# Moving the light heads' elementwise products from GpSimd to VectorE in a fused MoE, attention, MoE kernel

## The chip, the cores and the metric

The kernel runs on one core of a Trainium2 chip. Its metric is device time in microseconds (us) from the start to the end of one execution. TensorE is PE in the rows (PEld its weight loads), VectorE is DVE, ScalarE is ACT, GpSimd is POOL, SyncE is SP.

## The reference

The input x has 8 batches of 512 rows of 128 channels. Three residual stages follow one another:

```python
x = x + 0.5 * ffn(layernorm(x))      # 8 experts of 512 hidden units, the best one of each row
x = x + attention(layernorm(x))      # 16 heads of 8 channels, values are the keys, gated
x = x + 0.5 * ffn(layernorm(x))

windows = [max(4, 128 // 2 ** h) for h in range(16)]
mask = (j <= i) & (j > i - windows[h])
att = softmax(where(mask, q @ k.T / sqrt(8), -inf))
combined = att @ v                   # v = k
gates = softmax(x @ Wgate + bgate)   # one gate for each head
out = (combined * gates) @ Wproj + bproj
```

Head h looks back over a window of 128, 64, 32, 16, 8, 4, 4, ... keys. The four widest are called dense and the twelve others light.

## The kernel before

The program is one block with an instruction stream for each engine; their order is written out by hand and semaphores connect them. An expert stage sorts the rows by expert (scatter by indirect DMAs from GpSimd's queue, L481), computes 46 blocks of 128 rows in pairs (`ffn`, L1258 and L1267), and brings the rows back.

The attention stage goes through 8 batches of 4 tiles, and each batch i through 7 slots n, written here as slot (i, n). The dense heads go through TensorE: scores of unit n (L1343, L1345), negated maximum on VectorE (`dense_max`, L973 and L977), exponentials on ScalarE (L691, L694), transposes (L1355), copy (L704) and products with the values (`outputs`, L1370 to L1377). TensorE and VectorE work two units ahead of the slot (`ahead(i, n, 2)`), so VectorE's maximum in slot (i, 0) is that of unit (i, 2).

The light heads do not use TensorE. The keys of a batch are written to DRAM and loaded back four rows' shifts at a time into `ks` and four more for the widest light head into `ks4` (SP, `keys`). Then:

- `light_products` (L325) multiplies the shifted keys with the queries: a small one for `ks4` (L332, 128x128) and a large one for `ks` (L334, 128x1536). It waits for the load of the keys and for `lsc_s` of the batch before, after which `prod` is free.
- `light_sums` (L980) and `light_scores` (L992) reduce the products to scores on VectorE, `light_probs` (L707, L710) takes the exponential on ScalarE.
- `light_parts` (L337) multiplies the shifted keys with these probabilities (L341, L345), the same two sizes. `light_outputs` (L1012) sums them (L1015 to L1019), and `gate` (L1022) scales all heads (L1026 to L1042) for the projection. TensorE's `outputs(i, 0)` of the next batch waits for `gated_s` from `gate`, as its bank is read there.

Before the change GpSimd runs `light_products` for batches 1 to 7 and `light_parts` for batches 0 to 6; VectorE runs `light_products` of batch 0 and `light_parts` of batch 7 itself. GpSimd's share of the attention stage is `window(i)`, in order: `light_products(i)`; `roots` (L528) in windows 1 and 3; `normalise_batch(i + 2)` (L322), which needs TensorE's `turn_batch(i + 1)` of slot (i, 0) (L1307); in window 1 `centre` and `squares` of tiles 20 to 31 (L514, L509), after VectorE's means in slot (1, 2); in windows 3 to 6 `roots` and `normalise` (L528, L356); in window 2 `add_output_bias` (L522, 128x2560); and `light_parts(i)`.

VectorE's slots are in `slot_of` (L1070): in slot (i, 0) the maximum, from batch 2 on row sums and centring of batch i - 2 (L797, L807), then `light_outputs(i - 1)`; in slot (i, 1) the maximum and `gate(i - 1)`; in slot (i, 3), or (7, 2) in the last batch, the maximum and `light_sums(i)`; in slot (i, 4) maximum, `add_bias` and `light_scores(i)`. `besides` holds single pieces of work for some slots; the routing of the last expert stage is computed in slots (6, 4), (6, 6) and (7, 1) (L861 to L909), and the scatters of that stage wait for it.

Of the kernel before, what the change touches and what calls it, by code (L numbers as in the profile page):

```python
# [5 lines left out]
B, T, C = 8, 512, 128  # L6
# [58 lines left out]
def macaron(nc, x_in, w_qkg, b_qkg, w_q4, w_k4, b_q4, b_k4, w_proj, b_proj, w_router, w_fc, w_out, consts, out):  # L65
# [4 lines left out]
    with ctx:  # L70
# [3 lines left out]
        def sem(name):  # L74
            return ctx.enter_context(nc.semaphore(name))
# [140 lines left out]
        norm_s = sem("rows_normalised")  # L216
# [64 lines left out]
        def batch(i):  # L281
            return slice(4 * i, 4 * i + 4)
# [182 lines left out]
        def _(pool):  # L465
# [62 lines left out]
                pool.tensor_tensor(rstd[:, tiles], var[:, tiles], minus_half[:, 0:len_of(tiles)], ALU.pow).then_inc(root_s, 1)  # L528

            def window(i):  # L530
                if i > 0:
                    light_products(pool, i, i % 2)
                if i in (1, 3):
                    roots(i // 2 + 1, LN2[i // 2 + 1])
                if i + 2 < B:
                    normalise_batch(pool, i + 2)
                if i == 1:
                    centre(LN2[2])
                    squares(6, LN2[2])
                if 3 <= i < 7:  # L540
                    roots(i, batch(i - 3))
                    normalise(pool, 1, (root_s, i), batch(i - 3))
                if i == 2:
                    add_output_bias(6, slice(LN2[1].start, N_TILES))
                if i + 1 < B:
                    light_parts(pool, i, i % 2)

            pool.wait_ge(zero_s, 48)
            scatter(0, 0, SEG[0][0], 1)
# [237 lines left out]
        def _(dve):  # L787
# [58 lines left out]
            def spread(n, tiles):  # L846
                root_guess(n, tiles)
                for k in range(3):
                    root_step(tiles, last=k == 2)
# [203 lines left out]
            def half_attended(i):  # L1053
# [2 lines left out]


            besides = {
                (0, 2): lambda: light_products(nc.vector, 0, 0),
                (0, 0): lambda: residual(LN2[1], 4), (0, 1): lambda: row_sums(LN2[1]), (0, 3): lambda: centre(LN2[1]),  # L1060
                (0, 5): lambda: variance(5, LN2[1]), (0, 6): lambda: scaled_variance(5, LN2[1]),
                (1, 1): lambda: residual(LN2[2], 5), (1, 2): lambda: (row_sums(LN2[2]), means(LN2[2])),
# [7 lines left out]
            def slot_of(i, n):  # L1070
                nxt = ahead(i, n, 2)
                if nxt:
                    dense_max(*nxt)
                if i >= 2 and n == (0 if i + 1 < B else 4):

                    half_attended(i - 1)
                    row_sums(batch(i - 2))
                    if i == 2:

                        dve.wait_ge(cent_s, len(LN1) + len(LN2))  # L1080
                    centre(batch(i - 2))
                if i:
                    if n == 0:
                        light_outputs(i - 1)
                    if n == 1:
                        gate(i - 1)
                    if n == 6:
                        attended(i - 1)

                early = i + 1 == B  # L1090
                if n == 3 - early:
                    light_sums(i)
                if i + 1 < B:
                    if n in (2, 4):
                        add_bias(i + 1, n // 2 - 1)
                    if n == 5:
                        gate_logits(i + 1)
                if n == 4 - early:
                    light_scores(i)
                if i >= 2:  # L1100
                    if n == (4 if i == 2 else 2) and i + 1 < B:
                        variance(7 + i - 2, batch(i - 2))
                    if n == (6 if i == 2 else 5) and i < 6:
                        scaled_variance(7 + i - 2, batch(i - 2))
                if (i, n) in besides:
                    besides[i, n]()
# [69 lines left out]
            last = SEG[1][1]  # L1176

            spread(11, batch(4))
            normalise(nc.vector, 1, (rstd_s, len(SEG[0]) + 2), batch(4))
            gate(B - 1)  # L1180
            half_attended(B - 1)
# [353 lines left out]
```

## Time and profile before

| | |
|---|---|
| median of 3 runs | 498.62 us (497.4 to 502.13) |
| the profiled execution's own time | 496.32 us |
| its span, first to last instruction | 494.5 us |
| busy, of the span | PE 83%, DVE 67%, ACT 58%, POOL 48% |
| mean granted TensorE clock | 0.886 of full speed |
| attention stage | about 143 to 383 us |

Busy shares are averages over stages with different limits, so the attention stage is read by itself: the chain of waits shows what was waited for, and the timelines of each engine show which instruction took longer than others of its form. The times in a timeline are microseconds from the start of the span.

### The profile page before, as it was taken

Reading aid. Unit: us, or ns where it says so; the run is one execution under the profiler, and the core shown is the slowest. Engines: PE = TensorE matmul, PEld = TensorE weight load, DVE = VectorE, ACT = ScalarE, POOL = GpSimd, SP = SyncE. Lnnn points to the kernel's source line nnn. Section 1 sums busy time; section 2 is a strip of 40 time slices with the busy share of each in tenths; the row PEclk is TensorE's granted clock in tenths of the full one; section 3 lists DMA queues with packets and bytes.
Section 4 is the critical chain, followed back from the end, with each engine's and each line's share of the span. In section 5 each row is a group of like instructions: output and inputs, shape, how many; then the busy total and the mean of one; then the engine's idle time right before and its main releaser. Section 6 shows DMA issues by size and latency. Waiting matters only on the chain.

```text
span 494.5 us, 9979 instructions
## 1 busy us (share of the span) xinstructions
PE 408.2 (83%) x2828; PEld 381.5 (77%) x2837; DVE 330.3 (67%) x668; ACT 285.0 (58%) x875; POOL 235.2 (48%) x204
## 2 busy tenths in 40 slices
PE   2941999999977869959998989794887979989990
PEld 1940899999966868849797979693776969989990
DVE  5867344558754898895959696969894385545550
ACT  2330576767746647836868677753342746767660
POOL 4047760170227894651826252414375246777551
PEclk9999999999999767987979898876565799999997
DMA  8981332242216660522525322122023613362210
GB/s 254 407 227 59 98 115 64 77 125 74 64 34 136 138 158 13 124 50 64 109 63 110 81 70 74 15 50 37 33 98 105 179 36 107 104 177 63 62 42 0
DMA packets 85356, 48.16 MB, mean 97 GB/s; under 512 B 45874, under 2 KB 80314, under 8 KB 85073
## 3 DMA queue, kind: packets, MB, share of 16 engines
q1 hardware_dynamic: 80272, 37.32, 29.2%
q0 software_dynamic: 5056, 10.52, 6.8%
q8 instruction: 12, 0.20, 0.2%
q14 instruction: 16, 0.12, 0.1%
HBM read 25.66 MB, written 22.98 MB: 98 GB/s over the span
## 4 chain that ended last, share of the span: by engine, by line
PE 56%; DVE 20%; POOL 8%; issue 7%; ACT 3%; DMA 3%; POOLq 0%; DVEq 0%; SPq 0%; ACTq 0%
PE bank L1258 17%; PE bank L1267 17%; PE bank L1345 5%; POOL late_rows_d L481 4%; PE bank L1377 4%; DVE osh L1017 3%; PE bank L1326 3%; POOL rows_d L481 3%; PE bank L1249 2%; ACT late L694 2%; PE bank L1355 2%; DVE nmax L977 2%; PE bank L1233 2%; DMA xs<-late_rows_d 1%; DVE osh L1019 1%
## 5 line engine op out<-in xcount | busy, mean ns | idle before, releaser
L1267 PE MATMUL bank<-wo,hT 128*128 x736 | 101.6, 281 | 5.3 <-ACT hT L616 5.2
L915 DVE TENSOR_SCALAR hT<-bank 128x512 f32<-128x512 f32 x92 | 63.6, 691 | 59.5 <-PE bank L1258 58.9
L1258 PE MATMUL bank<-xT,fcb 128*128 128x128 f32 x736 | 101.1, 282 | 0.7 <-ACT xT L600 0.7
L1267 PEld LDWEIGHTS bank<-wo,hT 128*128 128x128 f32 x736 | 90.3, 193 | 6.6 <-issue 6.1
L1258 PEld LDWEIGHTS bank<-xT,fcb 128*128 128x128 f32 x736 | 93.2, 199 | 1.5 <-ACT xT L600 1.5
L610 ACT ACTIVATE fcb<-fc 128x512 f32 x92 | 57.7, 629 | 51.1 <-PE bank L1258 50.9
L616 ACT ACTIVATE hT<-hT 128x512 f32<-128x512 f32 x92 | 57.6, 626 | 10.1 <-DVE hT L915 9.9
L491 POOL DMA_INDIRECT out_rows<-late x46 | 45.3, 984 | 37.2 <-DVE late L924 30.4
L694 ACT ACTIVATE late<-bank,nmax 128x128 f32<-128x128 f32 (+1 forms) x128 | 50.0, 394 | 14.5 <-DVE nmax L977 13.6
L1345 PE MATMUL bank<-kT,qT 128*128 128x128 f32 (+4 forms) x256 | 54.2, 345 | 0.5
L704 ACT ACTIVATE PT<-bank 128x384 f32<-128x384 f32 (+1 forms) x56 | 28.6, 511 | 42.2 <-PE bank L1355 42.1
L1345 PEld LDWEIGHTS bank<-kT,qT 128*128 128x128 f32 x256 | 47.6, 219 | 3.2 <-issue 0.5
L977 DVE TENSOR_REDUCE nmax<-bank 128x1 f32<-128x256 f32 (+1 forms) x96 | 29.2, 345 | 31.1 <-PE bank L1345 30.4
L481 POOL DMA_INDIRECT rows_d<-rows,slot x32 | 32.5, 1016 | 34.2 <-DVE slot L909 25.1
L500 POOL DMA_INDIRECT late<-y_d,slot x32 | 32.0, 1000 | 35.0 <-DMA y_d<-ys 23.3
L481 POOL DMA_INDIRECT late_rows_d<-rows,slot x32 | 31.6, 986 | 27.5 <-DVE slot L909 18.4
L1233 PEld LDWEIGHTS bank<-wr,rT 128*128 128x128 f32 x128 | 28.5, 301 | 14.1 <-ACT rT L594 12.2
L1343 PE MATMUL bank<-maskb,identb 128*128 128x448 bf16 (+1 forms) x48 | 17.7, 369 | 25.5 <-ACT late L694 25.4
L600 ACT ACTIVATE xT<-bank 128x128 f32<-128x128 f32 x92 | 23.8, 261 | 18.3 <-PE bank L1249 18.2
L341 POOL TENSOR_TENSOR part<-ks,pl 128x128 f32<-128x128 f32 x7 | 3.0, 426 | 65.9 <-ACT pl L710 65.9
L1355 PE MATMUL bank<-cst,late 128*128 128x128 f32 x176 | 33.9, 311 | 0.0
L1377 PE MATMUL bank<-qkg,PT 128*128 128x8 f32 x192 | 33.6, 296 | 0.0
(133 smaller groups left out, 804.3 us busy)
## 6 DMA issues: line engine op xcount, KB each, us to landing
ks<-k_d SPq DMA_DIRECT2D x32, 192.0 KB, 3.3
late_rows_d<-hT SPq DMA_DIRECT2D x5, 1028.0 KB, 7.0
rows_d<-late SPq DMA_DIRECT2D x2, 1472.0 KB
xs<-rows_d SPq DMA_DIRECT2D x23, 128.0 KB
y_d<-ys SPq DMA_DIRECT2D x46, 64.0 KB
xs<-late_rows_d SPq DMA_DIRECT2D x23, 128.0 KB
late<-late_rows_d SPq DMA_DIRECT2D x2, 1225.5 KB, 6.9
fc<-in_w_fc SPq DMA_DIRECT2D x1, 2048.0 KB
```

The lines of the kernel that those rows point to most:

```text
L481: pool.indirect_dma_start(out=(late_rows_d if f else rows_d)[:, :], out_offset=bass.IndirectOffsetOnAxis(ap=slot[:, t:t + 1].bitcast(u32), ...
L491: pool.indirect_dma_start(out=out_rows, out_offset=bass.IndirectOffsetOnAxis(ap=xid[:, b, C:C + 1].bitcast(u32), axis=0), in_=xid[:, b, 0: ...
L610: act.activation(fcb[:, v, :], fc[:, ds(e, 1), :].rearrange("p e h -> p (e h)"), ACT.Copy)
L616: act.activation(block_h, block_h, ACT.Square).then_inc(hT_s, 1)
L694: act.activation(rows[:, to + 128 - w:to + 128], s[:, a0:a0 + w], ACT.Exp, bias=nmax[:, t, h:h + 1], accum_out=den[:, i % 2, t, h:h + 1]). ...
L915: nc.vector.tensor_scalar(hT[:, v, :, :].rearrange("p k c -> p (k c)"), bank[v][:, :], 0.0, None, ALU.max).then_inc(r_s, 1)
L977: mx = nc.vector.tensor_reduce(nmax[:, t, h:h + 1], s[:, a0:a0 + w], AX.X, ALU.max, negate=True)
L1258: mm = pe.matmul(bank[v][:, k * 128:(k + 1) * 128], fcb[:, v, k * 128:(k + 1) * 128], xT[:, v, :], start=True, stop=True)
L1267: mm = pe.matmul(bank[OUT_BANK[f] + v][:, 0:128], hT[:, v, k, :], wo[:, ds(e, 1), k, :], start=(k == 0), stop=(k == KT - 1))
L1345: mm = pe.matmul(s[:, a0:a0 + w], qT[:, u, h, t * 128:(t + 1) * 128], kT[:, u, (t + 1) * 128 - w:(t + 1) * 128], start=False, stop=h == he ...
L1355: mm = pe.transpose(bank[3][:, c * 128:(c + 1) * 128], P[:, (n + 1) // 2 % 2, k, :], ident)
L1377: mm = pe.matmul(o(h, h + 1), PT[:, t % 2, h + 1, :], v(t, h), start=(t == 0), stop=(t == 0 or h == DENSE - 1))
```

## The change

VectorE runs `light_products` and `light_parts` for all 8 batches. `light_products(i)` stands in slot (i, 3), or (7, 2), right ahead of `light_sums(i)`, and that of batch 0 moves from slot (0, 2) to (0, 3). `light_parts(i - 1)` stands in slot (i, 0), right ahead of `light_outputs(i - 1)`. GpSimd's windows lose both calls; everything else in them keeps its order. One wait on `norm_s` is added after the attention loop on VectorE.

```diff
             def window(i):
-                if i > 0:
-                    light_products(pool, i, i % 2)
                 if i in (1, 3):
                     roots(i // 2 + 1, LN2[i // 2 + 1])
                 if i + 2 < B:
@@
                 if i == 2:
                     add_output_bias(6, slice(LN2[1].start, N_TILES))
-                if i + 1 < B:
-                    light_parts(pool, i, i % 2)
@@
             besides = {
-                (0, 2): lambda: light_products(nc.vector, 0, 0),
@@
                 if i:
                     if n == 0:
+                        light_parts(nc.vector, i - 1, (i - 1) % 2)
                         light_outputs(i - 1)
@@
                 if n == 3 - early:
+                    light_products(nc.vector, i, i % 2)
                     light_sums(i)
@@
             spread(11, batch(4))
+            dve.wait_ge(norm_s, 6)
             normalise(nc.vector, 1, (rstd_s, len(SEG[0]) + 2), batch(4))
```

## Rows read from the trace of the kernel before

**Rows 1.** Page, chain that ended last, by engine
```profile
PE 56%; DVE 20%; POOL 8%; issue 7%; ACT 3%; DMA 3%; POOLq 0%; DVEq 0%; SPq 0%; ACTq 0%
```

**Rows 2.** Busy time by stretch, batches 2, 5, 6: us, busy (count), PEclk, DMA share, GB/s
```profile
204.50:236.00 31.50, 25.14 (x155) 22.87 (x156) 26.24 (x41) 18.39 (x74) 14.23 (x7) 0.84 0.34 75
...
283.20:307.00 23.80, 21.60 (x147) 19.33 (x147) 19.42 (x39) 17.73 (x71) 10.20 (x8) 0.93 0.26 60
307.00:343.60 36.60, 29.43 (x171) 25.93 (x171) 31.34 (x54) 19.27 (x75) 13.99 (x9) 0.78 0.25 50
```

**Rows 3.** Timeline of TensorE in batch 5
```profile
284.71 0.60 PE L1307 MATMUL bank<-cst,xb 128*128 128x128 f32 x4
...
293.97 0.36 PE L1371 MATMUL bank<-qkg,PT 128*128 128x8 f32 x2 [0.69 <-DVE fcb L1042]
```

**Rows 4.** Timeline of VectorE in batch 5, in brackets the idle time before
```profile
288.88 1.27 DVE L1019 TENSOR_TENSOR osh<-osh,o 128x32 f32<-128x32 f32 x1
...
300.31 0.54 DVE L977 TENSOR_REDUCE nmax<-bank 128x1 f32<-128x160 f32 x2 [2.15 <-PE bank L1345]
```

**Rows 5.** Source lines of three small VectorE instructions, eight of each
```profile
L1019 DVE TENSOR_TENSOR osh<-osh,o x8: 192/654/2726, 185.3 to 365.9; 128x32 f32<-128x32 f32 x8
L1037 DVE TENSOR_TENSOR fcb<-osh,fac x8: 557/558/1282, 189.1 to 371.1; 128x384 f32<-128x384 f32 x8
L1030 DVE TENSOR_TENSOR dg<-den,gsum x8: 224/226/5090, 188.0 to 370.0; 128x64 f32<-128x64 f32 x8
```

**Rows 6.** Timeline of GpSimd in batch 5
```profile
286.64 3.46 POOL L334 TENSOR_TENSOR prod<-ks,qkg 128x1536 f32<-128x1536 f32 x1
...
292.16 1.06 POOL L356 TENSOR_TENSOR rows<-rows,rstd 128x512 f32<-128x512 f32 x1
```

**Rows 7.** Source lines of the large products on both engines: duration ns min/median/max, starts
```profile
L334 POOL TENSOR_TENSOR prod<-ks,qkg x7: 3440/3462/3509, 181.4 to 337.7; 128x1536 f32<-128x1536 f32 x7
L334 DVE TENSOR_TENSOR prod<-ks,qkg x1: 1748/1748/1748, 163.5 to 163.5; 128x1536 f32<-128x1536 f32 x1
```

**Rows 8.** Timeline of VectorE, parts of batch 7: start us, us, instruction
```profile
360.03 0.29 DVE L341 TENSOR_TENSOR part<-ks,pl 128x128 f32<-128x128 f32 x1
360.23 1.75 DVE L345 TENSOR_TENSOR part<-ks,pl 128x1536 f32<-128x1536 f32 x1
```

**Rows 9.** Timeline of VectorE in slots (1, 3), (1, 4) and (1, 5)
```profile
194.43 0.68 DVE L977 TENSOR_REDUCE nmax<-bank 128x1 f32<-128x256 f32 x2
...
197.84 0.54 DVE L977 TENSOR_REDUCE nmax<-bank 128x1 f32<-128x160 f32 x2 [0.37 <-PE bank L1345]
...
200.52 0.68 DVE L973 TENSOR_REDUCE nmax<-bank 128x4 f32<-128x512 f32 x1
```

**Rows 10.** Timeline of VectorE, the centring of slot (5, 0)
```profile
284.35 0.69 DVE L807 SCALAR_TENSOR_TENSOR rows<-rowsum,rows 128x512 f32<-128x512 f32 x1
```

**Rows 11.** Timeline of VectorE, the maximum of slot (1, 1)
```profile
186.93 0.69 DVE L977 TENSOR_REDUCE nmax<-bank 128x1 f32<-128x256 f32 x2 [1.47 <-PE bank L1345]
```

**Rows 12.** Timeline of GpSimd in batches 1 and 2
```profile
194.60 2.76 POOL L514 TENSOR_TENSOR rows<-rows,rowsum 128x1536 f32<-128x1536 f32 x1 [7.00 <-DVE rowsum L801]
197.44 2.75 POOL L509 TENSOR_TENSOR sq<-rows 128x1536 f32<-128x1536 f32 x1
...
212.37 5.20 POOL L522 TENSOR_TENSOR rows<-rows,bproj 128x2560 f32<-128x2560 f32 x1
```

**Rows 13.** Timeline of ScalarE, first exponential of unit (2, 0)
```profile
202.08 0.36 ACT L694 ACTIVATE late<-bank,nmax 128x128 f32<-128x128 f32 x1
```

**Rows 14.** Timeline of VectorE, slots (2, 6), (6, 5) and (6, 6)
```profile
234.87 1.20 DVE L844 TENSOR_SCALAR var<-var 128x4 f32<-128x4 f32 x1
...
332.67 2.87 DVE L1006 TENSOR_TENSOR gl<-qkg,gmax 128x64 f32<-128x64 f32 x1
...
337.98 3.28 DVE L880 TENSOR_TENSOR n_tok<-upto,before 128x8 f32<-128x8 f32 x1
```

**Rows 15.** Timeline of GpSimd, an indirect DMA while VectorE ran L334
```profile
164.05 1.98 POOL L500 DMA_INDIRECT late<-y_d,slot  x1 [0.30 <-issue]
```

## The prediction

> **What bounds the kernel now.** I read the page's chain first, then the chain of waits through the attention stage, then the timelines of four engines side by side, batch by batch. The chain is TensorE for 56% and VectorE for 20% [rows 1]. The expert stages hold nothing that the change touches, so only the stretch from about 143 to 383 us can move. There an undisturbed batch takes 23.6 to 23.8 us; batch 2 takes 31.5 and batch 6, with the routing in it, 36.6 [rows 2]. In batch 5 TensorE is busy 21.6 us of 23.8 and VectorE 19.4 [rows 2]: neither is free, and they alternate. VectorE carries the chain from the maximum of slot (i, 0) to the end of `gate` in slot (i, 1), without a pause; TensorE carries it from `outputs(i, 0)`, which had waited 0.69 us for `gate` [rows 3], through slot (i, 4), where VectorE idles 2.15 us for it [rows 4].
>
> The reader should also see that VectorE's small instructions are sometimes very long. L1019 takes 0.19 us at best and 2.73 at worst, L1030 takes 0.22 and once 5.09, L1037 takes 0.56 or 1.28 [rows 5]. Each long one ends where a GpSimd instruction ends: L1019 at 290.15 [rows 4] with L334 at 290.10 [rows 6]. So an instruction with two tensors in SBUF waits on VectorE for GpSimd's running one. The Trainium skill has this as a rule (SBUF — State Buffer, section "Who interferes with whom"): the pair of ports is an exclusive lock, and whoever starts first keeps it for the whole instruction. The trace agrees, with 1.27 us for the L1019 at 288.88 where 0.19 is its least.
>
> **The change part by part.** GpSimd loses 7 large products L334 of 3.46 us [rows 7] and 7 somewhat shorter L345, with their small ones. It is not on the chain except in the scatters, so this time is itself worth nothing; what counts is what it blocked.
>
> VectorE gains 14 pairs. A pair costs 0.2 us for the small one (360.03 to 360.23) and 1.75 for the large one, 1.95 us [rows 8]; L334 is 1.75 there too [rows 7]. That is 27 us of work on VectorE. The seven `light_parts` stand in slot (i, 0), inside the stretch that carries the chain, and count in full. The seven `light_products` stand in slot (i, 3): where VectorE idles 2.15 us afterwards [rows 4] they are hidden (without that cover each would cost 1.95); batch 1 has only 0.37 us [rows 9] and the last batch next to none.
>
> GpSimd's other work moves forward. Its `normalise_batch` now starts as soon as `turn_batch` ends, at 285.31 in batch 5 [rows 3], and would find VectorE's large L345 running since about 285.2 (the centring L807 ahead ends near 285.0 [rows 10], plus 0.2 for L341). It waits, then runs under the reductions L1015 to L1017, which take one tensor and were not lengthened anywhere. With L528 and L356 behind it (some 3.1 us together) it is through before L1019. So in the batches without other work both L1019 and L1037 run at their shortest.
>
> The running sum, as delay of the chain:
>
> - Batch 0: products only change places in the row, 0. The parts of batch 0 in slot (1, 0) fill an idle time of 1.47 us ahead of the maximum of slot (1, 1) [rows 11]; the 0.5 us left over is taken up by ScalarE's and TensorE's own order.
> - Batch 1, slot (1, 3), +5.4. VectorE's means release GpSimd's L514, 2.76 us, 0.17 us after the start of the last maximum before the products [rows 9, 12]. That maximum has 0.6 us to go, so L332 finds the ports taken. With VectorE 0.5 us late it waits from 195.5 to 197.8. Behind L514 stands L509, 2.75 us [rows 12]. If it takes the ports between L332 and L334, the products end near 202.5, the maximum of unit (1, 6) starts at 204.7 where it had 197.84, and that of (2, 0) at 206.9 where it had 200.52 [rows 9]. The first exponential of (2, 0) had 0.9 us to spare (202.08 against 201.20) [rows 9, 13]: 6.3 less 0.9 is 5.4. If L334 goes ahead of L509, the same working gives 3.8. I take 5.4, since L509 has by then waited longer.
> - Batch 2, -1.0. Before, L1019 lost 1.08 us and L1030 4.87 to L334 and to the bias of 5.20 us [rows 5, 12]. Now the bias follows `normalise_batch` and ends 7.8 us after `turn_batch`; L1019 loses about 2.4 and L1030 nothing. Parts 1.95 plus 2.4 less 5.95 is -1.6. TensorE, at its lower clock of 1.2 GHz after some 4 us of idle time in batch 1, brings `turn_batch` and so the bias 0.6 us later: -1.0.
> - Batch 2, clock, -0.9. At a granted clock of 0.84 it had 25.14 us of matmuls [rows 2]; at batch 5's 0.93 these would be 22.7, so up to 2.4 us can come back when the single 4.8 us wait for L1030 is gone. TensorE would still idle near 1.7 us there, more than the 0.69 of batch 5 [rows 3], so I take a good third, 0.9.
> - Batch 3, +1.0: parts 1.95, less 0.95 of the 1.20 us of L844, which waited for GpSimd's L345 [rows 14]; TensorE's scores allow no more.
> - Batch 4, +0.4, and batch 5, +0.2: the maximum of slot (i, 1) comes 1.95 later less L1019's 1.1, and 0.69 of the rest was TensorE's wait for `gate` [rows 3], which L1037's 0.72 [rows 5] now makes earlier.
> - Batch 6, slots 0 and 1, -0.6: L1019's 2.73 falls to 0.19 [rows 5], parts 1.95.
> - Slots (6, 5) to (7, 1), -1.65. L1006 loses 2.65 us of its 2.87 and L880 3.1 of its 3.28 [rows 14], as both waited for GpSimd's light products. Scores allow the maximum behind L1006 to come 1.7 us sooner, so -1.7 - 3.1 + 1.95 = -2.85 for the slots that start the scatter. Then `light_products(7)` runs on VectorE just as the first scatter is issued. An indirect DMA that fell on L334 took 1.98 us, where its neighbours take 0.94 [rows 15]; I take 1.2 us for it. The Trainium skill warns of this only for two-port copies, and infers that tensor_tensor does not do it (same page and section); by the page it would be 0 and the sum 1.2 lower. The row decides for 1.2.
>
> The added wait on `norm_s` costs nothing: it stands for GpSimd's normalisations of windows 3 to 6, done by 340 us.
>
> Sum: 5.4 - 1.0 - 0.9 + 1.0 + 0.4 + 0.2 - 0.6 - 1.65 = +2.85, about 2.9 us. The span goes from 494.5 to 497.4, the profiled execution's time from 496.32 to 499.2. The median shown is 2.3 above that execution, so the median goes from 498.62 to 501.5.
>
> Lower bound of the terms: 3.8 in batch 1, -1.6 and -2.4 in batch 2, nothing lost in the scatter (-2.85): -2.0, or 496.6. Upper bound: see the first rival.
>
> **The rivals.**
>
> (a) GpSimd takes the ports first in slot (i, 0), slower. The margin between VectorE's L345 (285.2) and the end of `turn_batch` (285.31) [rows 3] is 0.1 us plus a semaphore's way. If `normalise_batch` wins, L345 waits 1.04 us in batches 3, 4 and 5: +3.1, to 504.6. If the bias in batch 2 follows at once, 5.20 us [rows 12], with L1019's 2.4 then free, that is up to 3.9 more: 508.5. It decides from 0.2 us on. For it: the margin is thin. Against it: L341 takes the ports 0.2 us before. 20%.
>
> (b) The cheap corner: L334 slips in before L509, the clock of batch 2 recovers, and the first scatter loses nothing. 496.6 to 499. For it: at 290.10 VectorE got the ports ahead of GpSimd's next instruction. 18%.
>
> (c) Faster: as (b), and TensorE, with fewer long waits, keeps the high clock in batch 6. Its 29.43 us at 0.78 [rows 2] would be 4.7 shorter at 0.93; with two thirds on the chain -2.0 - 3.1 = -5.1, 493.5. Against it: batch 6 keeps a wait of over 2 us. 8%.
>
> (d) 27 us of VectorE work cost more in slots that I hold covered, above all (4, 3) and (5, 3), where 1.95 stands against 2.15 less the shift of 0.2. Each uncovered 1 us in six batches: +6, 507. 6%.
>
> **How the numbers follow.** The forecast has 48%, with its own range 499 to 504. A measurement of this kernel tells about 1%, 5 us, from no change, that is outside 493.6 to 503.6. Faster by over 1%: (c) and a little, 10%. Slower: (a), (d) and the forecast's upper edge, 30%. Within 1%: 60%. The range 496.3 to 507.5 leaves out (c) and the top of (a).
>
> **What would show it.** L334 and L345 eight times each on VectorE, 1.75 us where not blocked. L332 or L334 long in slot (1, 3), and the period from 181 to the same point of batch 2 up by over 4 us. L1019 at 0.19 us in batches 3 to 6 and near 2.6 in batch 2; L1030, L1006 and L880 short. The idle time in slot (i, 4) of batches 4 and 5 close to zero. The first scatter longer than 1.5 us and 1 to 2 us nearer to the start of batch 7. A long L345 in slots (3, 0) to (5, 0) would prove (a). The prediction is wrong if slot (1, 3) is not blocked or if batch 2 comes out shorter by more than 4 us.

## The result, and the profile after

| | before | after |
|---|---|---|
| median | 499.36 us (4 runs, 497.4 to 502.13) | 508.25 us (4 runs, 506.51 to 509.4) |
| profiled execution, its span | 496.32, 494.5 us | 509.4, 507.6 us |
| busy: PE, DVE, ACT, POOL | 83, 67, 58, 48% | 81, 68, 56, 38% |
| mean granted TensorE clock | 0.886 | 0.874 |

The ratio is 1.0171, with a 95% interval of 1.011 to 1.0232: slower, by an amount that may lie on either side of 2%. 501.5 us had been forecast, and 508.25 lies outside the range of 496.3 to 507.5. Medians here are over all executions, while a ratio leaves out executions in a slower state, so the two can differ a little. The two profiled executions differ by 13.1 us, more than the 8.9 of the medians; what follows takes apart those 13.1. In `after` the lines from the window on are numbered 2 to 4 lower: L1015 is the L1019 of before, L1033 the L1037, L1343 the L1345.

The stretch is cut at the start of the maximum in slot (i, 0), which the forecast's terms use too. In microseconds:

| | before | after | difference | forecast |
|---|---|---|---|---|
| to slot (1, 0) | 180.96 | 182.37 | +1.4 | 0 |
| batch 1 | 23.53 | 27.24 | +3.7 | +5.4 (or 3.8) |
| batch 2 | 31.49 | 29.59 | -1.9 | -1.9 (-1.0 and -0.9) |
| batch 3 | 23.6 | 27.16 | +3.6 | +1.0 |
| batch 4 | 23.6 | 27.22 | +3.6 | +0.4 |
| batch 5 | 23.76 | 27.23 | +3.5 | +0.2 |
| batch 6 | 36.69 | 31.36 | -5.3 | -5.4 (-0.6, -1.7, -3.1) |
| slot (7, 0) to the last scatter | 34.70 | 38.91 | +4.2 | +3.15 (1.95, 1.2) |
| from there to the end | 116.2 | 116.5 | +0.3 | 0 |

So the surprise is in batches 3 to 5, the ones without extra work: 10.7 us where 1.6 had been forecast. All other rows together are 1.2 us beside the forecast, but only as a sum: +1.4 ahead of slot (1, 0), -1.7 in batch 1 and +1.1 at the scatters are in it.

The stretches of after, by the view of busy time by windows (us, busy time and count of each engine, granted clock, DMA share, GB/s), answer to [rows 2]. Batches 2, 5 and 6, then batch 5 in three parts:

```profile
209.60:239.20 29.60, 25.20 (x146) 23.03 (x147) 25.19 (x44) 17.78 (x71) 9.79 (x3) 0.77 0.39 85
...
293.60:320.80 27.20, 24.60 (x146) 22.42 (x146) 21.55 (x42) 17.65 (x71) 6.42 (x5) 0.81 0.30 67
320.80:352.20 31.40, 28.18 (x171) 25.65 (x171) 26.23 (x59) 19.10 (x75) 0.00 (x0) 0.84 0.22 39
293.60:303.60 10.00, 7.85 (x52) 6.46 (x52) 9.72 (x17) 6.91 (x27) 4.37 (x3) 1.00 0.44 90
303.60:314.60 11.00, 11.00 (x48) 10.39 (x49) 8.39 (x18) 5.71 (x21) 0.00 (x0) 0.55 0.00 1
314.60:320.80 6.20, 5.76 (x48) 5.57 (x47) 3.44 (x9) 5.03 (x24) 2.05 (x2) 0.98 0.60 148
```

Batch 5 of before, cut into parts by what the clock does:

```profile
283.20:293.20 10.00, 8.76 (x56) 7.11 (x55) 9.72 (x16) 7.81 (x29) 7.90 (x6) 1.00 0.49 108
293.20:296.70 3.50, 2.81 (x25) 2.76 (x25) 3.50 (x10) 2.23 (x10) 0.01 (x1) 0.99 0.00 0
296.70:300.20 3.50, 3.50 (x16) 3.24 (x15) 1.43 (x2) 2.17 (x8) 0.00 (x0) 0.52 0.01 2
300.20:306.90 6.70, 6.43 (x55) 6.12 (x53) 4.71 (x12) 5.42 (x25) 2.19 (x2) 1.00 0.19 46
```

Before, TensorE ran at 0.52 of full speed, its level of 1.2 GHz, for 3.5 us of the batch. After, it did so for 11 us (0.55), and 11.00 of these 11.00 us were busy: slow, not waiting. The timelines of TensorE show the same matmuls at both speeds. Before (start, us, instruction, in brackets the idle time ahead and its releaser):

```profile
292.17 0.36 PE L1343 MATMUL bank<-maskb,identb 128*128 128x448 bf16 x1 [1.24 <-ACT late L694]
...
294.19 0.81 PE L1377 MATMUL bank<-qkg,PT 128*128 128x8 f32 x6
```

After:

```profile
303.48 0.36 PE L1341 MATMUL bank<-maskb,identb 128*128 128x448 bf16 x1 [2.15 <-ACT late L690]
...
304.90 1.43 PE L1375 MATMUL bank<-qkg,PT 128*128 128x8 f32 x6
```

The six small products take 1.43 us where they took 0.81. What came ahead of them is a wait of 2.15 us where it was 1.24: ScalarE's exponential is released by VectorE's maximum, which stands behind the parts in the row. The page's chain answers to [rows 1]; it has two points less of TensorE's share, now of a longer span, and still TensorE first:

```profile
PE 54%; DVE 19%; POOL 9%; issue 7%; DMA 5%; ACT 3%; POOLq 0%; SPq 0%; DVEq 0%; ACTq 0%
```

VectorE's source lines L1015, L1033, L1026 and L345 (duration in ns: least, median, greatest) answer to [rows 5, 8]:

```profile
L1015 DVE TENSOR_TENSOR osh<-osh,o x8: 191/193/2130, 188.7 to 377.3; 128x32 f32<-128x32 f32 x8
L1033 DVE TENSOR_TENSOR fcb<-osh,fac x8: 557/559/561, 191.0 to 382.6; 128x384 f32<-128x384 f32 x8
L1026 DVE TENSOR_TENSOR dg<-den,gsum x8: 224/225/227, 189.9 to 381.5; 128x64 f32<-128x64 f32 x8
L345 DVE TENSOR_TENSOR part<-ks,pl x8: 1751/1752/1754, 183.0 to 371.7; 128x1536 f32<-128x1536 f32 x8
```

Of these four lines only one L1015 is blocked, in batch 2. In batches 3 to 5 the change did on VectorE what it had been expected to do, and the time still went up by more than VectorE can account for.

### The profile page after: what moved, and what is told of

Its sections match the earlier page's. It is cut to its first block, busy times and chain, and to the rows that moved or that the text cites. A ratio compares the mean times of both kernels' runs of the same rounds, so it can differ in the third digit from the quotient of the medians.

```text
span 507.6 us, 9979 instructions
## 1 busy us (share of the span) xinstructions
PE 413.7 (81%) x2828; PEld 387.5 (76%) x2837; DVE 342.7 (68%) x696; ACT 286.0 (56%) x875; POOL 194.9 (38%) x176
## 4 chain that ended last, share of the span: by engine, by line
PE 54%; DVE 19%; POOL 9%; issue 7%; DMA 5%; ACT 3%; POOLq 0%; SPq 0%; DVEq 0%; ACTq 0%
PE bank L1265 15%; PE bank L1256 15%; PE bank L1343 5%; POOL late_rows_d L481 4%; PE bank L1375 4%; DVE osh L1013 3%; PE bank L1247 2%; POOL rows_d L481 2%; PE bank L1353 2%; DMA xs<-late_rows_d 2%; PE bank L1324 2%; DVE part L345 2%; ACT late L690 2%; DVE nmax L973 2%; DVE rowsum L793 2%
## 5 line engine op out<-in xcount | busy, mean ns | idle before, releaser
L612 ACT ACTIVATE hT<-hT 128x512 f32<-128x512 f32 x92 | 57.6, 626 | 10.7 <-DVE hT L911 10.5
L481 POOL DMA_INDIRECT late_rows_d<-rows,slot x32 | 33.8, 1056 | 60.5 <-DVE slot L905 51.3
L1343 PE MATMUL bank<-kT,qT 128*128 128x128 f32 (+4 forms) x256 | 54.4, 346 | 1.4 <-ACT late L690 0.5
L1343 PEld LDWEIGHTS bank<-kT,qT 128*128 128x128 f32 x256 | 48.0, 220 | 3.4 <-issue 0.2
L973 DVE TENSOR_REDUCE nmax<-bank 128x1 f32<-128x256 f32 (+1 forms) x96 | 29.3, 348 | 28.6 <-PE bank L1343 27.9
L500 POOL DMA_INDIRECT late<-y_d,slot x32 | 32.6, 1018 | 35.3 <-DMA y_d<-ys 23.6
L481 POOL DMA_INDIRECT rows_d<-rows,slot x32 | 32.5, 1016 | 34.3 <-DVE slot L905 25.1
L322 POOL TENSOR_TENSOR xb<-rows,rstd 128x512 f32<-128x512 f32 x7 | 12.6, 1794 | 72.3 <-PE bank L1305 61.1
L1231 PEld LDWEIGHTS bank<-wr,rT 128*128 128x128 f32 x128 | 28.5, 301 | 14.5 <-ACT rT L590 12.7
L1341 PEld LDWEIGHTS bank<-maskb,identb 128*128 128x128 bf16 x56 | 6.9, 122 | 40.4 <-ACT late L690 37.8
L1375 PE MATMUL bank<-qkg,PT 128*128 128x8 f32 x192 | 35.8, 308 | 0.0
```

Source lines behind the costliest of these rows:

```text
L481: pool.indirect_dma_start(out=(late_rows_d if f else rows_d)[:, :], out_offset=bass.IndirectOffsetOnAxis(ap=slot[:, t:t + 1].bitcast(u32), ...
L612: act.activation(block_h, block_h, ACT.Square).then_inc(hT_s, 1)
L973: mx = nc.vector.tensor_reduce(nmax[:, t, h:h + 1], s[:, a0:a0 + w], AX.X, ALU.max, negate=True)
L1343: mm = pe.matmul(s[:, a0:a0 + w], qT[:, u, h, t * 128:(t + 1) * 128], kT[:, u, (t + 1) * 128 - w:(t + 1) * 128], start=False, stop=h == he ...
L1375: mm = pe.matmul(o(h, h + 1), PT[:, t % 2, h + 1, :], v(t, h), start=(t == 0), stop=(t == 0 or h == DENSE - 1))
```

## The experiments

Theory 1, formed on these traces: the maximum of slot (i, 1) comes some 0.9 us later, TensorE's wait for it grows from 1.2 to 2.2 us, and after the longer wait the chip grants 1.2 GHz for some 10 us rather than 3.5. This is worth 3.3 us in each of batches 3 to 5. (Batch 3 of before does not fit it well: it was at the lower level for 7 us after a wait of 1.14 us, batch 4 for 3.5 us after 1.10 us.) Theory 2, the rival: the moved work costs on VectorE itself (1.95 us a batch, plus products that the idle time in slot (i, 3) does not cover). All runs were compared with the kernel before on the same chip, whose median there was 498.96, 500.48 or 500.65 us. "Periods" are the times between the cuts of the table above, for batches 1 to 6; those of before are 23.5, 31.5, 23.6, 23.6, 23.8, 36.7 and those of after 27.2, 29.6, 27.2, 27.2, 27.2, 31.4.

**Filling TensorE's wait.** The change whole, and in slots (3, 2), (4, 2) and (5, 2) TensorE computes one projection of the keys three times, into its own bank, where once is enough. The result is the same and VectorE's row is untouched.

```diff
+AGAIN = {i + 1: 2 for i in (3, 4, 5)}
@@
             def dense_keys(i):
+                for _ in range(AGAIN.get(i, 0)):
+                    pe.matmul(bank[6][:, :], wk4[:, :], xnT[:, i % 2, :], start=True, stop=True)
                 pe.matmul(bank[6][:, :], wk4[:, :], xnT[:, i % 2, :], start=True, stop=True)
```

> The changed kernel; TensorE computes the dense keys of batches 4, 5 and 6 three times instead of once (two idle repeats, same result), in slots (3, 2) to (5, 2), where it otherwise idles 2.15 us for VectorE's late maximum. VectorE's work is untouched. Theory 1 (clock): the extra 3.5 us that batches 3, 4 and 5 each take come from TensorE's clock, which falls to 1.2 GHz for 10 us after that idle time. With the idle time filled to some 0.4 us, the granted clock stays at 1.00 for most of the batch, the period falls from 27.2 to 23.6 to 24.5 us and the time from 508 to 498 to 500. Theory 2 (VectorE bound): VectorE's 3.9 us of added work per batch set the period; nothing changes, 506 or more. Theory 3 (work on TensorE is full): the repeats cost 1.7 us per batch, 513.

497.48 us (496.2 to 499.61), ratio to before 1.0013 (0.9973 to 1.0052); periods 27.5, 29.7, 23.9, 24.0, 23.9, 31.3. The three batches are 3.2 to 3.3 us shorter again, and the others within 0.3 us of what they were. In the timeline of TensorE the wait of batch 5 is 0.43 us, and in the windows the slow stretch is gone but for a part of 7 us:

```profile
296.63 0.36 PE L1344 MATMUL bank<-maskb,identb 128*128 128x448 bf16 x1 [0.43 <-ACT late L691]
```

```profile
286.75:296.75 10.00, 9.57 (x56) 7.23 (x56) 9.72 (x17) 6.91 (x27) 4.36 (x3) 1.00 0.49 107
296.75:303.75 7.00, 7.00 (x44) 6.61 (x44) 6.90 (x14) 5.21 (x20) 0.00 (x0) 0.81 0.00 1
303.75:310.70 6.95, 6.68 (x53) 6.37 (x52) 4.89 (x14) 5.54 (x25) 2.05 (x2) 0.95 0.29 74
```

VectorE's busy time in the first 10 us, 9.72, is that of after. Theory 2 has no room for a gain of some 10 us from work added to TensorE, and theory 3 had forecast a loss. It is not wholly out for the rest: the batches take 23.9 us where those of before took 23.6 to 23.8.

**The delay alone.** The kernel before, with three idle reductions, 1.0 us together, put on VectorE in slots (3, 0) to (5, 0), where the parts would stand. Their result is not used.

```diff
+                if i in (3, 4, 5) and n == 0:
+                    for _ in range(3):
+                        step(nc.vector.tensor_reduce(top2[:, 0:20], tied[:, 0:20, :], AX.X, ALU.max))
                 if i:
                     if n == 0:
                         light_outputs(i - 1)
```

> The kernel before, with three idle reductions of 128x160 (0.32 us each, some 1.0 us together) on VectorE at the start of light_outputs in slots (3, 0), (4, 0) and (5, 0); none of the change is in it. Theory 1 (clock): 1.0 us more of waiting by TensorE lowers its clock for 10 us instead of 3.4, so each of the three batches becomes 3 to 4 us longer, the time 508 to 510. Theory 2 (each microsecond on VectorE costs one): 1.0 us for each, 502.5.

504.16 us (503.17 to 506.15), ratio 1.0112 (1.0066 to 1.0159); profiled span 504.0. Periods 23.6, 31.5, 26.4, 27.2, 27.2, 36.8. In the timeline of VectorE the three are one row, 1.02 us; then TensorE's wait, and the stretch behind it, which is that of after:

```profile
291.69 1.02 DVE L1084 TENSOR_REDUCE top<-tied 128x20 f32<-128x160 f32 x3
```

```profile
299.48 0.36 PE L1346 MATMUL bank<-maskb,identb 128*128 128x448 bf16 x1 [1.82 <-ACT late L694]
```

```profile
299.90:310.90 11.00, 10.39 (x47) 9.69 (x46) 6.31 (x16) 5.22 (x20) 0.00 (x0) 0.53 0.00 1
```

A delay of 1.0 us costs 2.8, 3.6 and 3.4 us in the three batches. The spans differ by 9.5 us as theory 1 has it; the medians by 5.2 only, less than the 508 to 510 us of theory 1 asks for. A likely reason shows in the next run.

**A third of the delay.** As above with one reduction, 0.35 us.

```diff
-                    for _ in range(3):
+                    for _ in range(1):
```

> The kernel before with one idle reduction (0.32 us, some 0.35 us with its wait) on VectorE in slots (3, 0), (4, 0) and (5, 0), where three cost 2.8 to 3.6 us a batch. Theory 1 (clock, a step): TensorE's wait grows from 1.24 to 1.5 us; if it stays on the near side of the step the batches grow by 0.3 us each, total +1, 500; if it crosses, by 3 each, 508. Theory 2 (the loss grows in proportion to the delay): about 1.1 us each, 502.

502.28 us (496.15 to 504.77), ratio 0.9987 (0.9943 to 1.0032): not told from no delay. But the profiled execution, span 501.0, has periods of 22.7, 32.2, 26.2, 27.1, 25.3, 34.3, so that batches 3 to 5 are 2.6, 3.5 and 1.5 us longer, not the 1.1 each of theory 2 and not the even 0.3 or 3 of theory 1. In its batch 4 TensorE waited 1.20 us for the maximum and 0.76 for `gate`, which is near the 1.24 and 0.69 of before in batch 5, and yet:

```profile
270.00:276.00 6.00, 4.03 (x23) 3.48 (x22) 5.83 (x17) 4.54 (x18) 1.68 (x2) 0.82 0.07 16
276.00:282.00 6.00, 6.00 (x26) 5.74 (x27) 1.79 (x2) 2.17 (x8) 0.00 (x0) 0.50 0.00 0
```

The clock is 0.50 for at least 6 us. The kernel before stands at an edge: with such waits the slow stretch is short in one execution and long in another. That fits a median of before 3 us above its profiled execution, and a smaller distance of medians than of spans. It fits also that over 47 executions of the kernel before, 492.1 to 505.4 us long, the time is the longer the lower the mean granted clock (a correlation of -0.73, worked out from their list). The wait's length alone does not decide, and what does is left open.

**The delay with the wait filled.** The three reductions, and the two more projections of the keys in the same batches.

```diff
+AGAIN = {i + 1: 2 for i in (3, 4, 5)}
@@
+                if i in (3, 4, 5) and n == 0:
+                    for _ in range(3):
+                        step(nc.vector.tensor_reduce(top2[:, 0:20], tied[:, 0:20, :], AX.X, ALU.max))
```

> The kernel before with both the 1.0 us of idle reductions on VectorE and two idle repeats of the dense keys' matmul on TensorE, in batches 3 to 5. Theory 1 (clock): the delay that cost 2.8 to 3.6 us a batch alone now costs 0 to 0.5, as the wait it makes is filled: batches of 23.9, 499 to 501. Theory 2 (the delay itself costs it): 504 or more, as without the repeats.

498.51 us (496.85 to 499.96), ratio 0.9963 (0.9936 to 0.9991). Periods 23.0, 31.5, 23.3, 24.1, 26.2, 35.0. In the profiled execution the three batches take 73.6 us, where they took 80.8 with the delay alone and 71.0 in the kernel before. Batches 3 and 4 are at a granted clock of 0.93. Batch 5 is at 0.87 and stays above the 23.9 us expected; its wait for `gate` is 0.92 us, where batch 4 has 0.69. In the median the delay that cost 1.1% is made good.

**One projection more, not two**, in the changed kernel.

```diff
-AGAIN = {i + 1: 2 for i in (3, 4, 5)}
+AGAIN = {i + 1: 1 for i in (3, 4, 5)}
```

> The changed kernel with one idle repeat of the dense keys' matmul in slots (3, 2) to (5, 2) instead of two: TensorE's wait ahead of the scores is cut from 2.15 us to about 1.3, much as in the kernel before (1.24). Theory 1 (clock, a step between 1.3 and 2.2 us of waiting): the clock behaves as before the change, short drops, and batches 3 to 5 take 23.8 to 24.2 us, time 498 to 500. If the loss went in proportion to the wait, the batches would stand near 25.8, time 504.

498.95 us (497.24 to 500.12), ratio 1.003 (0.9986 to 1.0075); periods 27.2, 29.5, 23.9, 23.9, 24.0, 31.2. Waits of 1.29 us gave the same periods as waits of 0.44, so the loss is not in proportion to the wait. This is the run to set beside the kernel before, whose waits were 1.1 to 1.2 us. Batch 5, in the view by windows:

```profile
293.20:317.20 24.00, 21.59 (x145) 19.38 (x145) 21.55 (x44) 17.63 (x69) 2.05 (x2) 0.93 0.23 46
```

Before, the same batch took 23.76 us at the same clock of 0.93 [rows 2]. At equal clock the change costs it 0.2 us, though VectorE is busy 21.55 us where it was 19.42.

**The same in the kernel before**, one projection more.

```diff
+AGAIN = {i + 1: 1 for i in (3, 4, 5)}
```

> The kernel before with one idle repeat of the dense keys' matmul in slots (3, 2) to (5, 2); it fills 0.86 of the 1.24 us wait. Theory 1 (clock): the 3 to 8 us at the lower clock that each of these batches still has are set off by that wait, so they fall to 22.5 to 23.6 us, up to 3 us in all. Otherwise no change, 498 to 501.

493.29 us (490.91 to 497.68), ratio 0.9852 (0.9808 to 0.9896): the kernel before lost time in this way too. The profiled execution (span 495.9) is the slowest of the four. It has periods of 21.2, 32.1, 21.1, 25.3, 27.6, 34.2, and its batches 3, 4 and 5 are one batch at three clocks:

```profile
237.80:258.80 21.00, 19.80 (x141) 17.22 (x140) 18.31 (x39) 16.96 (x66) 12.18 (x9) 1.00 0.39 90
258.80:284.10 25.30, 24.14 (x149) 21.21 (x149) 19.31 (x38) 17.80 (x72) 10.18 (x8) 0.87 0.43 93
284.10:311.70 27.60, 25.68 (x149) 22.83 (x148) 20.08 (x38) 17.78 (x71) 10.13 (x8) 0.81 0.28 66
```

21.0 us at a granted clock of 1.00, 25.3 at 0.87, 27.6 at 0.81, the last as long as a batch of after and without any of the moved work. Its waits are 0.78 us for the maximum and 0.92 for `gate`, both far below 2.15: a long wait is not needed for a long slow stretch. Filling gained 7.4 us on the kernel before and 9.3 (one projection) or 10.8 (two) on the changed one. So in medians it does not close the distance between the two: 493.29 against 498.95.

**Half of the change: the parts.** VectorE computes `light_parts`, GpSimd keeps the products.

```diff
-                if i + 1 < B:
-                    light_parts(pool, i, i % 2)
@@
                     if n == 0:
+                        light_parts(nc.vector, i - 1, (i - 1) % 2)
                         light_outputs(i - 1)
```

> Half of the change: light_parts on VectorE for all batches, light_products on GpSimd for batches 1 to 7 as before. Theory 1 (clock): the maximum of slot (i, 1) comes about 1.1 us later than before, as in the changed kernel, so batches 3 to 5 again take about 27 us; with batch 1 not hit by the blocked products the time is 507 to 512, no better than the whole change. Theory 2 (the products are what costs): close to the kernel before, 500 to 502.

511.28 us (507.29 to 514.63), ratio 1.0233 (1.0148 to 1.0318), profiled span 505.5; periods 23.6, 31.3, 27.3, 27.6, 27.2, 35.3. Batches 3 to 5 lose all that the whole change loses, with TensorE's waits at 2.19, 2.81 and 2.30 us. A part of batch 3:

```profile
246.00:257.00 11.00, 10.81 (x52) 10.08 (x53) 6.38 (x15) 5.43 (x22) 1.77 (x2) 0.57 0.01 1
```

**The other half: the products.** VectorE computes `light_products`, GpSimd keeps the parts.

```diff
-                if i > 0:
-                    light_products(pool, i, i % 2)
@@
-                (0, 2): lambda: light_products(nc.vector, 0, 0),
@@
                 if n == 3 - early:
+                    light_products(nc.vector, i, i % 2)
                     light_sums(i)
```

> The other half: light_products on VectorE for all batches, light_parts on GpSimd for batches 0 to 6 as before. Theory 1 (clock): nothing is added in slot (i, 0) and L1019 and L1037 no longer wait for GpSimd, so TensorE's wait for the maximum shrinks from 1.24 us to 0.2 and its clock stays high: batches 3 to 5 take 21.7 to 22.5 us instead of 23.6; batch 1 still loses 3 to 4 us to the blocked products, batches 2, 6 and 7 gain 3, 2.5 and 3. Time 489 to 493, faster than the kernel before. Theory 2 (the products are what costs): 506 or more.

489.67 us (487.02 to 491.24), ratio 0.9776 (0.9714 to 0.9839); periods 26.5, 28.3, 21.9, 23.6, 22.0, 30.2. This half alone makes the kernel 2.2% faster (1.6 to 2.9%). Batch 1 loses 3.0 us, batch 2 gains 3.2, batch 6 gains 6.5. Batch 4 missed the expected 22.5: no wait ahead of it is over 0.35 us, and its clock is still 0.86. The halves do not add up. Alone, the products shorten batches 3 to 5 by 3.5 us together; with the parts moved as well they shorten them by 0.4 (81.6 us against 82.1 in the run before). In the row of GpSimd the first scatter is long here too, as `light_products(7)` runs on VectorE:

```profile
343.91 2.40 POOL L481 DMA_INDIRECT late_rows_d<-rows,slot  x1 [18.43 <-DVE slot L907]
```

**Products of batches 2 to 6 on VectorE, of 1 and 7 on GpSimd.**

```diff
-                if i > 0:
+                if i in (1, 7):
                     light_products(pool, i, i % 2)
@@
                 if n == 3 - early:
+                    if i not in (1, 7):
+                        light_products(nc.vector, i, i % 2)
                     light_sums(i)
```

> Only light_products of batches 0 and 2 to 6 on VectorE; those of 1 and 7 and all light_parts but the last on GpSimd. It is the products-only kernel without its two losing places. Theory 1 (clock and ports): batch 1 goes back from 26.5 us to 23.6, the first scatter from 2.40 us to 1.08, batches 3 to 5 keep 22 to 23.6; the routing may wait for GpSimd's products of batch 7 again (3 us). 486 to 490. Theory 2 (the gain of the products-only kernel comes from elsewhere, such as fewer GpSimd instructions in all): less gain than it, 490 to 494.

488.1 us (486.02 to 490.25), ratio 0.9727 (0.966 to 0.9793); periods 23.7, 28.5, 22.6, 23.6, 23.6, 31.0. The loss in batch 1 is gone: 23.7 against 26.5. That is 2.8 us for the products in slot (1, 3). Batch 3 is at a granted clock of 1.00. Two parts of batch 4 show that also this kernel pays the clock, here after 1.38 us of waiting for the maximum:

```profile
264.39 0.36 PE L1345 MATMUL bank<-maskb,identb 128*128 128x448 bf16 x1 [1.38 <-ACT late L694]
```

```profile
262.00:268.00 6.00, 4.62 (x30) 4.00 (x30) 5.76 (x19) 4.43 (x18) 0.00 (x0) 0.90 0.39 71
268.00:274.00 6.00, 6.00 (x26) 5.73 (x28) 4.58 (x7) 2.60 (x9) 0.00 (x0) 0.53 0.00 0
```

Batch 5 has such a stretch with next to no wait ahead of it, so waits are not the only thing that brings it on:

```profile
287.99 0.36 PE L1345 MATMUL bank<-maskb,identb 128*128 128x448 bf16 x1 [0.18 <-ACT late L694]
```

```profile
292.00:298.00 6.00, 5.95 (x26) 5.65 (x27) 4.86 (x8) 2.92 (x10) 0.00 (x0) 0.54 0.01 1
```

**Only the products of batch 1 back to GpSimd**, the rest of the change kept.

```diff
             def window(i):
+                if i == 1:
+                    light_products(pool, i, i % 2)
@@
-                    light_products(nc.vector, i, i % 2)
+                    if i != 1:
+                        light_products(nc.vector, i, i % 2)
                     light_sums(i)
```

> The changed kernel with light_products of batch 1 alone back on GpSimd. Theory 1 (blocked ports): in slot (1, 3) L332 no longer waits 2.2 us for GpSimd's centring and VectorE has 1.95 us less to do, so batch 1 falls from 27.2 us to about 24 and the time by 3 to 4 us, to 504.5; batches 3 to 5 stay at 27.2. Theory 2 (the delay of batch 1 is absorbed later): less than 1.5 us gained.

506.96 us (505.55 to 507.4), ratio 1.0105 (1.0048 to 1.0163), span 503.8; periods 26.4, 28.6, 26.9, 27.0, 27.0, 31.2. Batch 1 gained 0.8 us, where the block in slot (1, 3) had been expected to give back some 3. The timelines of GpSimd and of VectorE show why: GpSimd's large product now met the parts that VectorE runs in slot (1, 0).

```profile
181.01 0.45 POOL L332 TENSOR_TENSOR prod<-ks,qkg 128x128 f32<-128x128 f32 x1 [3.42 <-DMA ks<-k_d]
181.42 3.43 POOL L334 TENSOR_TENSOR prod<-ks,qkg 128x1536 f32<-128x1536 f32 x1
```

```profile
182.15 2.85 DVE L341 TENSOR_TENSOR part<-ks,pl 128x128 f32<-128x128 f32 x1
```

L341, 0.28 us when free, waited for the ports until 184.8. One block was traded for another, and TensorE was at its lower level late in the batch too:

```profile
196.00:199.00 3.00, 3.00 (x12) 2.67 (x13) 2.97 (x6) 2.38 (x10) 0.54 (x1) 0.50 0.00 0
```

So this run does not isolate the price of slot (1, 3).

**The whole change with the waits of batches 2 to 6 filled.**

```diff
+AGAIN = {i + 1: 2 for i in (2, 3, 4, 5, 6)}
```

> The changed kernel with two idle repeats of the dense keys' matmul in batches 2 to 6, where the first kernel of this kind had them in 3 to 5. Theory 1 (clock): batch 6 (31.3 us, wait of 2.1 us) gains 3 us as the others did; batch 2 gains at most 1, as its wait of 4.1 us is only part filled. 494 to 497. If a longer wait in batch 2 leaves the clock low anyway, 496.

493.81 us (493.52 to 494.25), ratio 0.9877 (0.9845 to 0.9908); periods 27.6, 27.1, 23.2, 25.6, 23.9, 28.1. Batch 2 gains 2.5 us, where at most 1 had been expected, and batch 6 3.3 on after. Batch 4, with its wait filled to 0.45 us, takes 25.6 us at a clock of 0.87 here and 24.0 in the first run. A change that is 1.7% slower by itself is 1.2% faster with ten matmuls added that nobody needs. The kernel before with three of them is 1.5% faster, so this does not make the whole change worth taking.

**The best found.** Products of batches 0 and 2 to 6 on VectorE, everything else on GpSimd as before, one projection more in batches 2 to 5.

```diff
+AGAIN = {i + 1: 1 for i in (2, 3, 4, 5)}
@@
-                if i > 0:
+                if i in (1, 7):
                     light_products(pool, i, i % 2)
@@
                 if n == 3 - early:
+                    if i not in (1, 7):
+                        light_products(nc.vector, i, i % 2)
                     light_sums(i)
```

> light_products of batches 0 and 2 to 6 on VectorE, the rest on GpSimd, and one idle repeat of the dense keys' matmul in batches 2 to 5. In the kernel without repeats batches 4 and 5 still spend 6 us at the lower clock. Theory 1 (clock): with the repeat they fall from 23.6 to 22 us, 3 us in all, 485. If TensorE's own work bounds these batches, the repeat costs 0.9 us each: 490 to 491.

483.77 us (480.32 to 485.32), ratio 0.9688 (0.9652 to 0.9723), profiled span 478.3. Periods 22.0, 27.2, 22.7, 22.0, 20.7, 31.8. From within batch 3 to the start of batch 6 the clock is high nearly throughout:

```profile
236.00:258.00 22.00, 20.50 (x148) 17.97 (x147) 21.62 (x39) 17.80 (x69) 6.74 (x5) 1.00 0.33 72
258.00:280.00 22.00, 21.26 (x142) 18.73 (x140) 19.59 (x41) 16.48 (x68) 6.29 (x5) 0.92 0.41 86
280.00:302.00 22.00, 21.73 (x157) 19.34 (x156) 20.99 (x46) 18.99 (x73) 5.34 (x5) 1.00 0.37 82
```

## Why the prediction was wrong, step by step

**Batches 3 to 5: the step that failed.** "the maximum of slot (i, 1) comes 1.95 later less L1019's 1.1, and 0.69 of the rest was TensorE's wait": the shift was read rightly and priced wrongly. On VectorE it was as written. From the maximum of slot (5, 0) to the end of `gate` it took 10.83 us where it had taken 10.65, the forecast's 0.2. L1015 and L1033 ran at their shortest:

```profile
301.26 0.19 DVE L1015 TENSOR_TENSOR osh<-osh,o 128x32 f32<-128x32 f32 x1
...
303.65 0.56 DVE L1033 TENSOR_TENSOR fcb<-osh,fac 128x384 f32<-128x384 f32 x1
304.13 0.28 DVE L1038 TENSOR_TENSOR fcb<-bank,fac 128x128 f32<-128x128 f32 x1
...
313.27 0.54 DVE L973 TENSOR_REDUCE nmax<-bank 128x1 f32<-128x160 f32 x2 [2.51 <-PE bank L1343]
```

But TensorE then needed 8.86 us from the end of `gate` to the maximum that starts at 313.27, where it had needed 6.48, and from there to the next cut 7.54 us instead of 6.63: 0.2, 2.4 and 0.9 us are the 3.5 of the batch. The forecast had held TensorE's durations fixed and let only its starts move. It had named the 0.9 us of later maximum and the 0.69 us wait, not that the same 0.9 us lengthen a wait in the middle of TensorE's row. In the runs, filling that wait takes 9.8 us off the three batches without touching VectorE, and making it in the kernel before costs 9.9 us of period. The granted clock of a batch tells its length better than which kernel it is: at 0.93, 23.8 us before and 24.0 changed; at 0.81, 27.2 changed, 27.2 with the bare delay, 27.6 in the kernel before with nothing but a projection more. Between these levels it tells less: at 0.86 and 0.87 batches of 23.6 to 26.2 us were seen. At equal clock the forecast's 0.2 and 0.4 held; what failed is that the clock was taken as given: a loss by it stood at nothing in the sum, with no reason given. The Trainium skill says of another kernel (TensorE: Matmul & The Clock Gate, section "A second HAM failure mode: psum-queue depth-cycling") that short idle times of TensorE, coming often between groups of matmuls, move it between its two levels, and that throughput suffers though a single matmul at the high level is as fast as ever. The traces here agree: 1.0 us more of such a wait made batches of 27 us out of batches of 24.

The forecast had this term within reach. Rival (c) and the term of -0.9 in batch 2 priced what the clock gives back when waits go; nothing priced what it takes when a wait grows.

The idle time in slot (5, 4), forecast near zero, was 2.51 us in the row above. It was the mark to look at: VectorE had nothing to wait for there but a TensorE that had become slower. Neither of the two signs by which the forecast would have called itself wrong came: slot (1, 3) was blocked, and batch 2 was not over 4 us shorter.

**Batch 1: the mechanism right, the cheaper order of two.** VectorE's small product did find the ports taken, by GpSimd's L514, and took 2.48 us instead of 0.28. Then L334 went ahead of L509, which waited in its turn (2.75 us of work in 4.34):

```profile
196.98 2.48 DVE L332 TENSOR_TENSOR prod<-ks,qkg 128x128 f32<-128x128 f32 x1
199.39 1.75 DVE L334 TENSOR_TENSOR prod<-ks,qkg 128x1536 f32<-128x1536 f32 x1
```

```profile
196.55 2.76 POOL L514 TENSOR_TENSOR rows<-rows,rowsum 128x1536 f32<-128x1536 f32 x1 [8.87 <-DVE rowsum L797]
199.40 4.34 POOL L509 TENSOR_TENSOR sq<-rows 128x1536 f32<-128x1536 f32 x1
```

That was the working's 3.8, and it measured 3.7. The step "L509 has by then waited longer" failed. Rival (b)'s argument, that VectorE had once got the ports ahead of GpSimd's next instruction, held here. It does not hold everywhere: in batch 0, in both profiles, a small VectorE instruction (L996 before, L992 after) waited through two of GpSimd's in a row, L522 and L322, and took 4.47 and 4.89 us. The rest of rival (b) failed: the clock of batch 2 did not recover, and the first scatter did lose.

**Batch 2: the total right, by chance.** L1030 is no longer blocked (0.23 us at most) and L1015 lost 1.94 us (2.13 less 0.19) where 2.4 had been written, so that slot (2, 0) to the end of `gate` became 2.0 us shorter (12.80 for 14.80). The clock half did not come: the clock fell to 0.77, where 0.84 had been [rows 2], and from there to the maximum of slot (2, 4) TensorE took 0.6 us more. The last 0.5 us were gained where L844 had been blocked. The forecast had put that one, as -0.95, into batch 3, but the row stands at 234.87 [rows 14], ahead of the cut at 235.98; so batch 3 had a forecast of +1.95 by its own terms and batch 2 one of -2.85.

**Batch 6: the causes right, the total with some luck.** -5.3 for -5.4. L1002 and L876, the L1006 and L880 of before, which had waited for GpSimd's products [rows 14], are short. But the terms of -0.6, -1.7 and -3.1 measured -1.4, -0.8 and -3.2. In slot (6, 1) L1030 had been blocked too (1.02 us), which the forecast left out, and behind L1002 VectorE now waits 1.75 us for TensorE:

```profile
345.20 0.23 DVE L1002 TENSOR_TENSOR gl<-qkg,gmax 128x64 f32<-128x64 f32 x1
347.18 0.69 DVE L973 TENSOR_REDUCE nmax<-bank 128x1 f32<-128x256 f32 x2 [1.75 <-PE bank L1343]
...
349.62 0.17 DVE L876 TENSOR_TENSOR n_tok<-upto,before 128x8 f32<-128x8 f32 x1
```

**The scatters: one term missing.** From slot (7, 0) to the first scatter it took 11.85 us for 9.89, the 1.95 of the parts. The first one did fall on L334 and took 2.40 us (before, 1.08): +1.3 for the 1.2 written. A later one fell on the parts of batch 7, in slot (7, 5), and took 2.53 (before, 1.56): +1.0, for which the forecast had no term. Rows of GpSimd and, for the first, of VectorE:

```profile
364.02 2.40 POOL L481 DMA_INDIRECT late_rows_d<-rows,slot  x1 [44.69 <-DVE slot L905]
...
371.80 2.53 POOL L481 DMA_INDIRECT late_rows_d<-rows,slot  x1 [0.30 <-issue]
```

```profile
363.72 1.75 DVE L334 TENSOR_TENSOR prod<-ks,qkg 128x1536 f32<-128x1536 f32 x1
```

The choice to go by the row, rather than by what the Trainium skill says (SBUF — State Buffer, section "Who interferes with whom"), that a tensor_tensor was not seen to stall a DMA, with the reason inferred, was right: here it did, by 1.3 us. The run with the products alone has 2.40 in the same place without the moved parts, and the run that leaves the products of batch 7 on GpSimd has 1.08, so it belongs to L334.

**Rival (a), the race for the ports: refuted.** GpSimd's `normalise_batch` found L345 running in batches 2 to 5 (L345 never above 1.754 us) and took 2.35 us there instead of 1.04. **Rival (c)**'s high clock in batch 6 did not come: 0.84. **Rival (d)** had the time, 507, by another mechanism: the products in slot (i, 3) are covered, as the products alone make no batch of 3 to 5 longer. **+1.4 to slot (1, 0)** had no term. 1.0 of it was there before the attention stage began, where the change touches nothing.

What stays open: by which condition the clock falls, as slow stretches followed waits of 0.18 to 2.8 us; how the 8.9 us between the medians divide between it and the rest, as profiles show single executions (filled in both kernels, 5.7 us remain, with the changed kernel's batches profiled at 0.93, those of before at 1.00, 0.87 and 0.81); what the block in slot (1, 3) costs by itself (2.8 us by the two runs on the products, 0.8 by the run that met another block; both count VectorE's own 1.95 us with it); and whether the parts alone are slower than the whole change at all: their median is 3 us above it, their profiled span 2.1 below it, their four executions lie between 507.3 and 514.6 us, and the two intervals overlap.

## What to carry to other kernels

Before moving work onto an engine that TensorE waits for, price the move twice: by what it shifts, and by what a longer wait of TensorE does to the speed of all that follows it. Here 0.9 us of shift made 3.5 us of batch. A move that is two moves should be costed as two: the products stood in a slot with cover and gained 2.2%, the parts stood on the chain and lost 2.3%. Where a wait cannot be removed, matmuls repeated into a bank that is overwritten anyway can fill it: one in each of three batches took 7 us off the kernel before, one or two took 9 to 11 off the changed one.

## What the runs showed of the hardware

- The granted clock after a wait of TensorE, in batches of otherwise equal work: 0.52 for 3.5 us after 1.24 us, 0.55 for 11 us after 2.15 us, 0.53 for 11 us after 1.82 us. The slow stretch does not begin with the wait: in batch 5 it began about 1 us behind the end of the wait after the change, and 4.4 us behind it before. With 1.29 us and one matmul more ahead of it, the batch took 23.9 us, as with 0.44. Near the edge the same kernel falls on either side: 21.0, 25.3 and 27.6 us for three like batches of one execution; and 6 us at 0.54 came behind a wait of only 0.18 us.
- An indirect DMA of GpSimd took 1.56, 1.98, 2.40 and 2.53 us where a large elementwise product of two SBUF tensors (1.75 us) ran on VectorE, and 0.94 to 0.96 without. It ended 0.8 to 0.95 us behind that product each time.
- Who gets the ports between two GpSimd instructions that stand back to back was seen both ways: VectorE's L334 at 199.39 went ahead of GpSimd's L509 at 199.40, but VectorE's L992 at 173.79 took 4.89 us and ended only behind GpSimd's L522 and the L322 that followed it.
